# Metaformer block on one core: the diagonals of C made by ScalarE from loaded columns, six buffers for scanned states, an earlier convolution in the turn's chunk, and another form of the norm's shift

## What is computed

```
xz = norm(t) @ in_proj.T                      # x and z, 2048 channels each
for each direction (forward, and backward over the reversed tokens):
    xc    = conv4(x) + bias                   # depthwise, causal
    dt,B,C = split(xc @ xproj.T, 64, 16, 16)
    delta = softplus(clip(dt @ dtproj.T + b) + b);  u = clip(xc, -10, 10)
    h_n[t] = exp(delta[t] * A_n) * h_n[t-1] + delta[t] * u[t] * B_n[t]      # n = 0..15
    y[t]   = sum_n C_n[t] * h_n[t] + D * u[t]
out = ((y_fwd + y_bwd) * silu(z)) @ out_proj.T + t
```

## Time and profile before

| | us |
|---|---|
| three runs | 8293.36, 8297.58, 8300.15 |
| the profiled execution | 8293.36 |
| its span | 8291.6 |
| busy: PE, DVE, ACT, POOL | 7183.5, 7167.0, 5359.5, 6811.7 |
| mean granted TensorE clock, as a share of full | 0.945 |

### The profile page before, as it was taken

The page is one execution under the profiler, slowest core; times in us unless marked ns, Lnnn a source line. Parts: engine busy times, 40 slices in busy tenths (PEclk is TensorE's granted clock), DMA queues, the critical chain, the costliest instruction groups (busy, mean ns, idle before and its releaser), DMA issues. The chain is left out here.

```text
span 8291.6 us, 115137 instructions
## 1 busy us (share of the span) xinstructions
PE 7183.5 (87%) x32512; PEld 4451.9 (54%) x32512; DVE 7167.0 (86%) x7788; ACT 5359.5 (65%) x12512; POOL 6811.7 (82%) x2864
## 2 busy tenths in 40 slices
PE   6578998999989998977889998999899987779999
PEld 3244555555555555554555555555555555534444
DVE  6912999999999999999999999999999999934444
ACT  5643777777777777776777777777777776610000
POOL 5613999999999999999999999999999999921110
PEclk7789999999999999988999999999999998989999
DMA  3273232323232323221323232323232322154342
GB/s 96 67 208 133 66 117 66 120 66 116 67 119 68 116 67 116 69 97 42 106 78 131 77 126 77 130 78 126 78 130 81 122 98 83 45 199 142 132 142 75
DMA packets 540826, 844.01 MB, mean 102 GB/s; under 512 B 112576, under 2 KB 260032, under 8 KB 522816
## 3 DMA queue, kind: packets, MB, share of 16 engines
q1 hardware_dynamic: 540224, 837.03, 30.8%
HBM read 583.83 MB, written 253.02 MB: 101 GB/s over the span
## 5 line engine op out<-in xcount | busy, mean ns | idle before, releaser
L1175 POOL TENSOR_TENSOR scan_w<-scan_du,scan_bcast_b 128x2048 f32<-128x2048 f32 x1023 | 4633.7, 4541 | 3.6 <-DMA scan_bcast_b<-bc 3.6
L1227 DVE TENSOR_TENSOR_SCAN scan_h<-scan_da,scan_state,scan_w 128x512 f32<-128x512 f32 x2560 | 3168.8, 1273 | 36.7 <-ACT scan_da L1070 21.3
L1070 ACT ACTIVATE scan_da<-scan_delta,scan_prm 128x512 f32<-128x512 f32 x4096 | 2803.8, 685 | 0.0
L958 PE MATMUL scan_yT<-all_ident,scan_hc 128*128 128x128 f32 x10240 | 1515.2, 279 | 769.9 <-DVE scan_hc L1237 769.4
L958 PEld LDWEIGHTS scan_yT<-all_ident,scan_hc 128*128 128x128 f32 x10240 | 1184.8, 142 | 1450.1 <-DVE scan_hc L1237 1069.9
L1227 DVE TENSOR_TENSOR_SCAN scan_hs<-scan_da,scan_state,scan_w 128x512 f32<-128x512 f32 x1536 | 1899.9, 1259 | 57.9 <-PE scan_in_ps L854 40.5
L832 PE MATMUL scan_in_ps<-scan_hn,scan_win 128*128 128x512 f32 x3840 | 1730.8, 593 | 13.3 <-issue 13.3
L1237 DVE TENSOR_TENSOR scan_hc<-scan_h,scan_bcast_c 128x512 f32<-128x512 f32 x2560 | 1642.2, 671 | 35.8 <-ACT scan_state L1050 33.9
L1184 POOL TENSOR_TENSOR scan_hp<-scan_hs,scan_bcast_c 128x512 f32<-128x512 f32 x1024 | 1306.7, 1276 | 53.9 <-issue 48.4
L832 PEld LDWEIGHTS scan_in_ps<-scan_hn,scan_win 128*128 128x128 f32 x3840 | 693.1, 190 | 714.5 <-issue 714.5
L1050 ACT ACTIVATE scan_state<-scan_h 128x1 f32<-128x1 f32 x2560 | 433.5, 169 | 877.4 <-DVE scan_h L1227 870.6
(11 more groups left out here) (122 smaller groups left out, 6771.4 us busy)
## 6 DMA issues: line engine op xcount, KB each, us to landing
yT<-scan_y_out SPq DMA_DIRECT2D x257, 256.0 KB, 2.0
scan_win<-winx SPq DMA_DIRECT2D x128, 512.0 KB, 3.8
xc<-scan_xc_out SPq DMA_DIRECT2D x256, 256.0 KB, 2.0
scan_xc<-xc SPq DMA_DIRECT2D x256, 256.0 KB, 4.0
scan_bcast_b<-bc SPq DMA_DIRECT2D x64, 1024.0 KB, 7.7
scan_bcast_c<-bc SPq DMA_DIRECT2D x64, 1024.0 KB, 7.9
scan_win<-winz SPq DMA_DIRECT2D x128, 512.0 KB, 4.8
scan_x<-x_pad SPq DMA_DIRECT2D x128, 257.5 KB, 2.6
```

What stands on the lines that cost most here:

```text
L958: last = nc.tensor.matmul(yT[:, tb], hc_slot(b, n)[:, tb * P:(tb + 1) * P], ident[:], is_transpose=True, start=(i == 0 and tb == 0), stop= ...
L1070: nc.scalar.activation(da[:, n % 2], delta[:, s], ACT.Exp, scale=decay(b, n)).then_inc(S["exp_done"], 1)
L1175: nc.gpsimd.tensor_tensor(w[:, g], du[:, s].unsqueeze(1).to_broadcast([P, G, T]), bcast_b[:, g * G:(g + 1) * G], ALU.mult).then_inc(S["w_d ...
L1227: nc.vector.tensor_tensor_scan(flip(b, h_slot(b, n)), flip(b, da[:, n % 2]), flip(b, w[:, n // G, n % G]), state_of(b, n), ALU.mult, ALU.a ...
```

## The change

Five edits:

1. The diagonals of C (`c_diag`) are made by ScalarE: SyncE loads the two rows of C as columns, `c_col` (128 partitions x 4 values for each of the two states, one DMA each, 4 bytes a piece), right after the second of C's four broadcasts near a chunk's end; ScalarE makes eight 128x128 diagonals in the first unit of the chunk, two after da(3), two after da(8), two after da(9), two after da(11). GpSimd's two products (L1150) are gone.
2. `hs` has six tiles, one for each state of PN and TN; the slot of a state is fixed, and its scan waits for its own use in the unit before.
3. u and du have one buffer instead of two (the room for 2), and so ud moves from n = 10 to n = 5 on ScalarE, and GpSimd's next u waits for this unit's ud.
4. In units whose convolution runs ahead in the forward direction while the scan still goes backward (111 to 127), the table is `TURN`: convolution at 2, xc_copy at 7, projection at 8.
5. In n1 nmr is a tensor_scalar with one tensor operand and 1/std as the per-partition scalar.

```diff
-NHS = 4
+HS = {n: i for i, n in enumerate(PN + TN)}
...
-                nc.vector.scalar_tensor_tensor(nmr[:, i:i + 1], mv[:, i, 0:1], -1.0, rstd[:, i:i + 1], ALU.mult,
-                                               ALU.mult).then_inc(shift_ready, 1)
+                nc.vector.tensor_scalar(nmr[:, i:i + 1], mv[:, i, 0:1], rstd[:, i:i + 1], -1.0, ALU.mult,
+                                        ALU.mult).then_inc(shift_ready, 1)
...
-                return hs[:, (b * NSN + SN.index(n)) % NHS]
+                return hs[:, HS[n]]
...
+        TURN = dict(diag=1, conv=2, xc=7, proj=8)
...
-            return [(b + DB + 1, NORMAL)] if b + DB + 1 < NU else []
+            a = b + DB + 1
+            return [(a, TURN if back(b) and not back(a) else NORMAL)] if a < NU else []
...
+        C_DIAG_AT = (3, 3, 8, 8, 9, 9, 11, 11)
...
+            def load_c_columns(chunk):
+
+                if chunk:
+                    hold(sp, S["c_diag_done"], chunk * NTN * TB, S["passed"])
+                for k in range(NTN):
+                    src = bc_d[chunk % NCH, NS + TN[k]:NS + TN[k] + 1, :].rearrange("o (b p) -> p (o b)", p=P)
+                    sp.dma_start(c_col[:, k], src, allow_slow_non_contiguous=True).then_inc(S["c_col_loaded"], LOAD)
...
                     broadcast(chunk + 1, 1, 1)
+                    load_c_columns(chunk + 1)
...
+            def c_diagonal(b, k, tb):
+
+                if tb == 0:
+                    act.wait_ge(S["c_col_loaded"], (b // DB + 1) * NTN * LOAD)
+                    if b:
+                        act.wait_ge(S["h_turned_used"], (b - 1) * NTN + k + 1)
+                nc.scalar.activation(c_diag[:, k, tb], ident[:], ACT.Copy, scale=c_col[:, k, tb:tb + 1]
+                                     ).then_inc(S["c_diag_done"], 1)
...
-                    if n == 10:
+                    if n == 5:
...
-                if b % DB == 0:
-                    for k in range(NTN):
-                        make_diagonal(b, k)
...
-                hold(pool, S["ud_done"], b + 1, S["passed"])
+                hold(pool, S["ud_done"], b + 2, S["passed"])
...
-                if n in SN:
-                    g = b * NSN + SN.index(n) - NHS
-                    if g >= 0 and SN[g % NSN] in PN:
-                        dve.wait_ge(S["hp_done"], g // NSN * NP + PN.index(SN[g % NSN]) + 1 + NP)
-                    elif g >= 0:
-                        dve.wait_ge(S["h_turn_mm"], g // NSN * NTN + TN.index(SN[g % NSN]) + 1)
-                else:
+                if n in PN:
+                    dve.wait_ge(S["hp_done"], b * NP + PN.index(n) + 1)
+                elif n in TN and b:
+                    dve.wait_ge(S["h_turn_mm"], (b - 1) * NTN + TN.index(n) + 1)
+                elif n in VN:
```

More of the change, by code:

```diff
@@ L565, in stage_scan @@
         v = sc.sb("v", [P, T])
-        delta, u, du = (sc.sb(n, [P, 2, T]) for n in ("delta", "u", "du"))
+        delta, u, du = sc.sb("delta", [P, 2, T]), sc.sb("u", [P, T]), sc.sb("du", [P, T])
         ud = sc.sb("ud", [P, T])
@@ L569, in stage_scan @@
         hc = sc.sb("hc", [P, NOUT, T])
-        hs, hp = sc.sb("hs", [P, NHS, T]), sc.sb("hp", [P, NP, T])
+        hs, hp = sc.sb("hs", [P, NSN, T]), sc.sb("hp", [P, NP, T])
+        c_col = sc.sb("c_col", [P, NTN, TB])
         c_diag, h_turned = sc.sb("c_diag", [P, NTN, TB, P]), sc.sb("h_turned", [P, T])
@@ L584, in stage_scan @@
                  "scan_done", "hc_done", "h_saved", "hc_used", "hp_done", "hp_used", "yT_copied", "stored", "passed",
-                 "c_diag_done", "h_turn_mm", "h_turn_copied", "h_turned_used")
+                 "c_col_loaded", "c_diag_done", "h_turn_mm", "h_turn_copied", "h_turned_used")
         S = {n: sc.sem(n) for n in names}
@@ L738, in between @@
                 load_hn(1)
+                load_c_columns(0)
                 for c, g in ((0, 2), (1, 1), (0, 3), (1, 2), (1, 3)):
@@ L860, in add_turned @@
                 pe.wait_ge(S["h_turn_copied"], b * NTN + k + 1)
-                pe.wait_ge(S["c_diag_done"], b // DB * NTN + k + 1)
+                pe.wait_ge(S["c_diag_done"], (b // DB * NTN + k + 1) * TB)
                 for tb in range(TB):
@@ L1073, in unit @@
                         proj_copy(b // DB + 1)
+                    if b % DB == 0:
+                        for i, at in enumerate(C_DIAG_AT):
+                            if n == at:
+                                c_diagonal(b, i // TB, i % TB)
                     for a, when in ins:
@@ L1101, in unit @@
                         act.wait_ge(S["yT_copied"], b + 1)
-                        nc.scalar.activation(ud[:], u[:, s], ACT.Copy,
+                        nc.scalar.activation(ud[:], u[:], ACT.Copy,
                                              scale=skip[:, block_of(b):block_of(b) + 1]).then_inc(S["ud_done"], 1)
@@ L1143, in _ @@
         def _(pool):
-            def make_diagonal(b, k):
-                n = TN[k]
-                pool.wait_ge(c_loaded[n // G], (b // DB + 1) * LOAD)
-                if b:
-                    pool.wait_ge(S["h_turned_used"], (b - 1) * NTN + k + 1)
-                nc.gpsimd.tensor_tensor(c_diag[:, k], bcast_c[:, n].rearrange("p (b t) -> p b t", t=P),
-                                        ident[:].unsqueeze(1).to_broadcast([P, TB, P]), ALU.mult
-                                        ).then_inc(S["c_diag_done"], 1)
             def scan_input(b):
@@ L1157, in scan_input @@
                 pool.wait_ge(p_in[s], (b // 2 + 1) * (NPL * LOAD))
-                hold(pool, S["ud_done"], b + 1, S["passed"])
-                nc.gpsimd.tensor_scalar(u[:, s], xc[:, s], 10.0, -10.0, ALU.min, ALU.max).then_inc(S["u_done"], 1)
+                hold(pool, S["ud_done"], b + 2, S["passed"])
+                nc.gpsimd.tensor_scalar(u[:], xc[:, s], 10.0, -10.0, ALU.min, ALU.max).then_inc(S["u_done"], 1)
                 pool.wait_ge(S["u_done"], b + 1)
                 pool.wait_ge(S["delta_done"], b + 1)
-                nc.gpsimd.tensor_tensor(du[:, s], delta[:, s], u[:, s], ALU.mult).then_inc(S["du_done"], 1)
+                nc.gpsimd.tensor_tensor(du[:], delta[:, s], u[:], ALU.mult).then_inc(S["du_done"], 1)
             def weigh_b(b, g, single=False):
-                s = b % 2
                 pool.wait_ge(S["du_done"], b + 1)
@@ L1171, in weigh_b @@
                     for i in range(G):
-                        nc.gpsimd.tensor_tensor(w[:, g, i], du[:, s], bcast_b[:, g * G + i],
+                        nc.gpsimd.tensor_tensor(w[:, g, i], du[:], bcast_b[:, g * G + i],
                                                 ALU.mult).then_inc(S["w_done"], 1)
                 else:
-                    nc.gpsimd.tensor_tensor(w[:, g], du[:, s].unsqueeze(1).to_broadcast([P, G, T]),
+                    nc.gpsimd.tensor_tensor(w[:, g], du[:].unsqueeze(1).to_broadcast([P, G, T]),
                                             bcast_b[:, g * G:(g + 1) * G], ALU.mult).then_inc(S["w_done"], G)
```

## The result

The changed kernel takes 8227.71 us (median of 4 runs, 8217.32 to 8232.23), the kernel before 8298.86 us beside it (4 runs, 8293.36 to 8303.61): a ratio of 0.9913, 95% interval 0.9896 to 0.9930. That is 71 us less, where 25 us were forecast. The profiled execution took 8232.23 us, its span is 8230.4.

The account below looks back on a forecast made before the run. The prediction took VectorE, with ScalarE and TensorE behind it, to set the pace, GpSimd following with little slack. From 8293.4 us its terms, -9 - 25 - 9 + 0 + 13 + 10 - 5 = -25, gave 8268 us, range 8231 to 8305.

Parts of the forecast that it names:

- Norm's shift, -9 us: First stage: ScalarE's 12.5 us of waits for the shift go, partly showing up elsewhere; -9 us, bounds -12.5 and 0.
- Turn's chunk, -25 us: Chunk where the scan turns: earlier convolution shortens ScalarE's and VectorE's waits, 436 to 411 us; -25 us.
- Six buffers elsewhere, -9 us: Scan loop outside the turn's chunk: VectorE's 10.3 us of waits for TensorE's turn go; -9 us, bounds -14 and 0.
- ud at step 5, +10 us: ScalarE in every unit: the earlier step uses up the slack, costing 0.05 us a unit; +10 us, bounds 0 and 146.
- TensorE's clock backward, -5 us: Backward units: a later convolution splits TensorE's idle 2 us, so its clock falls less often; -5 us, 0 to -15.
- Diagonals off GpSimd, 0 us: Chunk starts: 40 us of GpSimd's time removed only adds slack while VectorE is slower; 0 us, lower bound -37.
- GpSimd sets the pace: Rival for ordinary chunks: the diagonals' 2.50 us count in each, 37 us more gained, 8231 us; chance 0.15.
- The early convolution only moves the wait: Rival for the turn's chunk: VectorE loses at scan 8 what it lost at scan 11; 8293 us; chance 0.20.
- ScalarE becomes the one: Rival for all units: early ud delays da and VectorE waits for ScalarE; 8318 us at 0.25 us a unit; chance 0.12.
- +13 us for the load: Seven forward chunk changes: ScalarE's diagonals wait for C's columns, scan 4 starts 1.9 us late; +13 us, bounds 0 and 51.

Follow-up runs that it names:

- b_norm: Kernel before with only the norm's shift as a tensor_scalar: 8274.97 us, ratio 0.9974.
- a_again2: Changed kernel with one ScalarE pass done three times on every fourth tile of the first stage (2.4 us of delay): 8248.10 us, ratio 0.9938.
- a_hs4: Changed kernel with the ring of four buffers for scanned states back: 8316.53 us, ratio 1.0024 to the kernel before.
- b_hs5: Kernel before with five scanned-state buffers instead of four: 8258.77 us, ratio 0.9954.
- b_ud: Kernel before with ScalarE's u times D at step 5 instead of 10: 8336.08 us, ratio 1.0044.
- a_ud8: Changed kernel with ud at step 8 instead of 5: 8234.26 us, ratio 0.9923 to the kernel before.
- b_cdiag: Kernel before with only C's diagonals made on ScalarE from the loaded columns: 8308.98 us, ratio 1.0011.
- a_pdiag: Changed kernel with C's diagonals back on GpSimd and no load of columns: 8228.65 us, ratio 0.9919 to the kernel before.
- a_pgate: Changed kernel with C's diagonals back on GpSimd and the forward convolution waiting for the copy of z: 8229.64 us, ratio 0.9917 to the kernel before.
- a_gate: Changed kernel where a forward unit's convolution also waits for ScalarE's copy of z: 8212.26 us, ratio 0.9895 to the kernel before.
- b_gate: Kernel before where a forward unit's convolution also waits for ScalarE's copy of z: 8307.96 us, ratio 1.0008.

## Why the prediction was wrong

The sign was right, the size was not: -25 forecast, -71 measured (-61 between the two profiled spans), and the time lies 3 us under the range. What failed is the sizing of the waits. The norm's shift was taken at -9 us and is -23; the backward chunks 0 to 6 were to gain some 4 us by buffers, ud and clock together, and gain 24; the columns' load was taken at +13 and the seven forward chunks are only 5 us longer. Behind these stands one step: each part was priced by the listed waits that it ends, against what bound the kernel before.

- **"Norm's shift, -9 us", bounds -12.5 and 0**: b_norm shows -23 by the medians and -27 in the stage. The mechanism held: the successor takes 212 to 216 ns in all 32 places, beside GpSimd's additions too. The Trainium skill (SBUF — State Buffer, Who interferes with whom) lists tensor_scalar among those that can block, under conditions on the operands; this [128x1] form did not in any of 32. The same section's sentence on two SBUF inputs fits the 1940 ns of the old form. The lower bound was false: I took the sum of waits for the most that could go, but behind the wait TensorE's clock was at 1.2 GHz (a_again2 shows that a longer delay brings it down), and the slow matmuls were on the same path. "TensorE's queue and the loads are near" was a reason to take less, and the queue was the reason for more.
- **"Turn's chunk, -25 us"**: 25.6 measured, and that it fits is luck. The new unit came out much as drawn: the convolution starts 5.4 or 6.0 us behind the unit's first scan (5.5 by the forecast, 10.7 before), and VectorE waits 9.8 / 16 = 0.6 us a unit for da, at scan 8 (0.8 forecast). But the working rests on a convolution that ends earlier; that alone gives nothing (a_hs4, 436.4). I had put the 29.4 us of buffer waits "in this term" and priced only the convolution; one buffer gives 17 us, and the table then 8.5.
- **"Six buffers elsewhere, -9 us"**, bounds -14 and 0: mis-sized, and not a term of its own. In the changed kernel they are worth, with the turn's chunk, 89 us (a_hs4), since ud at step 5 needs them; added to the kernel before, even one is worth 37 us (b_hs5), 17 in the turn's chunk and 1.3 a chunk backward.
- **"ud at step 5, +10 us"**: with four buffers it costs 38 us (b_ud), with six it gains 2.0 a backward chunk, 6.5 by the medians (a_ud8). So the sign depends on the buffers. The 0.05 us a unit is right (24.84 against 24.79 us); what was left out is what ud does to TensorE's queue, for worse with four buffers (scan 11) and for better with six (the clock).
- **"TensorE's clock backward, -5 us", 0 to -15**: right in kind, the drops are gone; 2.0 us a chunk by a_ud8, about -14 for the seven.
- **"Diagonals off GpSimd, 0 us"**: right for the kernel before (b_cdiag), wrong for the changed one, where they are worth 2.8 us a backward chunk (a_pdiag) and 1.4 forward once the drops are gone (a_pgate). In the changed kernel's own time this can't be seen: a_pdiag's median is 0.9 us higher, its loop 10.7 longer and its other stages 15 shorter, and no run tells why. I priced each part against the old bound, and the bound moved.
- **The rivals**: "GpSimd sets the pace" (0.15) holds as soon as the other waits are gone. That its 8231 lies 3 us from the measured time is luck: it has 2.5 us less in every chunk, and the forward chunks got 0.7 longer. "The early convolution only moves the wait" (0.20) has the size of a_hs4, not its cause: the wait at scan 11 didn't move, because it was for a buffer. "ScalarE becomes the one" with ud (0.12) has the sign of b_ud, but the waits that grow there are for TensorE's turn and the saved state, not for da. Buffers that are freed late stood in no rival.
- **"+13 us for the load"**: over-priced. Of the 10.9 us in 8 places 6.5 are one wait at the loop's start; the seven of the forward chunks are 0.4 to 0.8 us each, 4.4 in all, against the 1.5 taken, and these chunks are 0.7 us longer than before. The pieces take 0.395 us, not 0.3, and b_cdiag's backward chunks show no cost of them (402.7 against 402.9).

Added up in the changed kernel: -26.5 in the first stage, +5 between it and the loop, -50.5 in the loop (-19 in chunks 2 to 6, -25.6 at the turn, +4.7 in the seven forward ones, -10 in the first two and the last), +10.6 behind: -61.

## What to carry to other kernels

Price a set of edits together: take the next bound's own cadence for every stretch (here GpSimd's, 399.5 us a chunk without the diagonals, 402 with them) and let all waits above it go, rather than adding what each edit gives against the old bound. A buffer that is released by a full in-order queue deserves to be tried first, and by one more at a time. And where the clock falls behind a pause, the pause can cost more than its length, and an added wait can pay if the clock then stays up (a_gate), but only where it doesn't hold a buffer (b_gate).

## What the hardware did that I had not expected

- A 1.83 us wait cost 4.4 us in the first stage, with matmuls at 1.2 GHz behind it, and an added wait on TensorE made the kernel 15 us faster (a_gate).
- The output stage, the same code in all, took 1046.4 to 1052.7 us in the profiles of the ten kernels that load C's columns and 1040.9 to 1047.3 us in those of the nine that don't. The means are 6 us apart, and no run tells why.
